# Four chained attention layers on one core: statistics and queue order changed in the second and third layer

## The chip, the cores and the metric

The kernel runs on one core of a Trainium2 chip. The metric is the device time of one execution in microseconds (us). The core has engines that run side by side, each with its own queue of instructions taken strictly in order: TensorE (PE in the rows; its weight loads are PEld), VectorE (DVE), ScalarE (ACT), GpSimd (POOL) and SyncE (SP), which issues transfers. They meet only through semaphores: an instruction that waits holds up all that is queued behind it on its engine.

## The reference, cut to what matters

Input `x` (8, 256, 512) passes through four layers; `u` is a context of the same shape. The first layer (attention) and the fourth are not touched by the change; nor is the third layer's last part (a feed-forward block).

Second layer, for each batch element (a recurrent block, 32 heads of size 16):

```python
xa = ln(x); sx = shifted(xa) - xa
t = tanh((xa + sx*maa_x) @ maa_w1)            # then five mixtures m = t @ maa_w2
xw, xk, xv, xr, xg = (xa + sx*(maa_j + m_j))  # five inputs
w = exp(-exp(time_decay + tanh(xw @ decay_w1) @ decay_w2))
r, k, v, g = xr@Wr.T, xk@Wk.T, xv@Wv.T, silu(xg@Wg.T)
s = k v' + w s ; out = r (faaaa k v' + s)     # a scan over 256 positions
x = x + (groupnorm(out)*gn_w + gn_b) * g @ Wo.T
xc = ln(x); kk = relu(xk2 @ fWk.T)**2; x = x + sigmoid(xr2 @ fWr.T) * (kk @ fWv.T)
```

Third layer: two attentions with 16 heads of 32, the first over `x` itself, the second with keys and values from `u`, each `x + softmax(mask(q k'/sqrt(32))) v @ Wo` after a layer norm of `x`.

## The kernel before, in words

The program runs the layers one after the other; each stage clears its semaphores and meets at a barrier. Nothing of one stage lies beside another.

**Second layer (`l1_layer`).** The 8 batch elements are pipelined by an order written out by hand, one list for each engine. In step b of `ALL` (-1 to 8) three elements are in work: p = b+1 is being prepared (norm, mixtures, projections), b is being scanned in 8 units (`PER`), and c = b-1 is finished (group norm, `Wo`, second norm, feed-forward part). VectorE does for each unit a `spread` (L1535, k times v), a `scan` (L1543) and a `receive` (L1551, times r), with the other operations of p and c between them at fixed places. TensorE's `picks(n)` (L1040) sums a unit's result. All of TensorE's other outputs go through a ring of six PSUM banks in the order of the list `ring`: each label waits until the label six places before it was drained.

The norm of element p: VectorE's `stats(p)` (L729, L733) behind scan 8b; then GpSimd's `deviations` with four instructions (L1009 variance plus eps, L1010 minus the mean, L1012 the power -1/2, L1014 their product); then ScalarE's `normed(p)` (L1271); TensorE turns it (L1088); ScalarE's `turned(p)` (L1281) writes `xa`; VectorE's `shift(p)` (L1561) behind scan 8b+1 needs it. Then ScalarE's `first_part` (L1290), VectorE's `first_input` (L1565), TensorE's `first` (L1096, L1098) and ScalarE's `tanh` (L1299), and the mixtures (L1109, L1315). The norm of c goes the same way: `add_out` (L1620) and `stats_c` behind scan 8b+3, `deviations`, `normed_c` (L1381), the turn, `turned_c` (L1391), `shift_c` (L1633) behind scan 8b+4, `shifts_c` (L1399) and `key_input` (L1637). Its group norm: `centre` (L1144), `squares` (L1365), `variances` (L1151), `roots` (L1375), `inverse` (L1596), `spread_rs` (L1160), `scale_y` (L1604). `out_part` (L1648, L1652) closes the step. `bonus_v` (L1589) needs TensorE's `bonus` (L1056).

**Third layer's attentions (`l2_attentions`).** 16 slots (element, first or second attention), each with 4 groups of 4 heads: 64 steps k. `product_of(k)` gives each step one product of 512 by 256 in two halves: k, v, q of the next slot, then the output product p of the slot before (L1994, L1998). TensorE's step: product half 0, scores(k+1) (L1933), weigh_values(k-2) (L1968), probabilities of k-1 turned for heads 0 and 1 (L1944), product half 1, heads 2 and 3, the sums turned (L1953), and in 24 of the 64 steps a block of normed `x` or of `u` turned for a later slot (`turn_in`, L2016). ScalarE does exponentials (L2042), copies the turned probabilities out (L2049), drains the products k and q (L2066) and the turned `u` (L2077). VectorE does mask (L2121), maxima (L2128), reciprocals (L2135), outputs (L2142), products v and p (L2156, L2159), the turned `x` (L2187) and the norms. These TensorE outputs use a ring of four banks: the second half of a product has the bank of its first half.

## Time and profile before

| what | value |
|---|---|
| time, median of 3 runs | 4052.76 us (4042.41 to 4058.26) |
| the profiled execution, its own time | 4049.53 us |
| its span in the profile | 4047.7 us |
| busy shares of the span | TensorE 86%, VectorE 57%, ScalarE 41%, GpSimd 7% |
| second layer, from its first scan to the end of its last | 1585.1 to 2526.9 us |
| its six steps with all three elements in work (b = 1 to 6) | 1683.6 to 2441.8 us |
| third layer's attentions, from about the third step on | 2640 to 3495 us |

All times in the rows are us from the span's start unless marked ns. PEclk is the clock that TensorE was granted, as a share of 2.4 GHz; the other level is 1.2 GHz. Matmuls in f32 are recorded in two pieces each, so 8 matmuls count x16. Pieces overlap their neighbours slightly, so start to start is the measure of what one costs in a queue.

### The profile page before, as it was taken

What the parts mean: (1) busy time and instruction counts of PE and PEld (TensorE: products, weight loads), DVE (VectorE), ACT (ScalarE), POOL (GpSimd) and SP (SyncE); (2) the same over time, 40 slices, a digit from 0 to 9 for tenths busy, and PEclk for the clock granted to TensorE, in tenths of its full rate; (3) what the DMA queues carried; (4) which work ended last, traced back from release to release, by engine and by line L of the source; (5) the groups of instructions that cost most, each with busy time, mean ns of one, the idle gap of its engine ahead of it and who ended that gap; (6) DMA issues with size and microseconds to landing.
All of it is one profiled execution on the core that took longest, in us unless ns stands there. A gap on an engine that the chain in (4) does not pass through costs nothing. (4 is left out here: it accounts for less than half of the span.)

```text
span 4047.7 us, 52713 instructions
## 1 busy us (share of the span) xinstructions
PE 3495.5 (86%) x20272; PEld 2497.6 (62%) x20272; DVE 2314.6 (57%) x3706; ACT 1667.4 (41%) x3920; POOL 299.5 (7%) x352
## 2 busy tenths in 40 slices
PE   7999999999999936688787976688888888699987
PEld 6777777778777715455454653365555555377764
DVE  5655555555655554887777888255555555442213
ACT  4454444444444423334434342155555555332211
POOL 0000000000000001011101110000000000000000
PEclk9999999999999977898888888799999999799998
DMA  5323121311221025333333333300000000110013
GB/s 195 138 84 121 68 105 74 115 63 63 97 92 63 32 96 165 94 74 89 84 84 88 69 87 75 125 24 6 6 14 19 27 14 14 64 60 27 26 38 104
DMA packets 91123, 291.69 MB, mean 72 GB/s; under 512 B 19872, under 2 KB 28064, under 8 KB 66304
## 3 DMA queue, kind: packets, MB, share of 16 engines
q1 hardware_dynamic: 63152, 182.55, 15.3%
q0 software_dynamic: 10368, 75.50, 5.0%
q10 hardware_dynamic: 17360, 30.32, 2.1%
q8 instruction: 162, 2.65, 0.3%
q14 instruction: 81, 0.66, 0.1%
HBM read 233.82 MB, written 54.53 MB: 71 GB/s over the span
## 5 line engine op out<-in xcount | busy, mean ns | idle before, releaser
L447 ACT ACTIVATE l_prob<-l_bank,l_nmax 128x512 f32<-128x512 f32 x512 | 345.3, 687 | 214.7 <-DVE l_nmax L527 214.7
L527 DVE TENSOR_REDUCE l_nmax<-l_bank 128x1 f32<-128x512 f32 x512 | 318.1, 684 | 80.3 <-PE l_bank L375 80.3
L344 PE MATMUL l_bank<-l_x_hi,l_w_hi 128*128 128x256 f32 x1024 | 316.3, 309 | 16.0 <-DVE l_x_lo L582 16.0
L2042 ACT ACTIVATE l2a_sc<-l2a_sc,l2a_nmax 128x256 f32<-128x256 f32 x512 | 254.5, 506 | 106.2 <-DVE l2a_nmax L2128 106.2
L344 PE MATMUL l_bank<-l_x_hi,l_w_lo 128*128 128x256 f32 x1024 | 291.1, 284 | 0.0
L344 PE MATMUL l_bank<-l_x_lo,l_w_hi 128*128 128x256 f32 x1024 | 291.1, 284 | 0.0
L1543 DVE TENSOR_TENSOR_SCAN l_kv<-l_wx,l_kv 128x2056 f32<-128x2056 f32 x64 | 283.8, 4434 | 3.1 <-ACT l_wx L1265 3.1
L550 DVE COPY l_probT<-l_bank 128x512 f32<-128x512 f32 x256 | 173.8, 689 | 178.5 <-PE l_bank L389 177.3
L389 PE MATMUL l_bank<-l_ident,l_prob 128*128 128x128 f32 x2048 | 248.9, 276 | 11.6 <-DVE l_q_lo L535 6.6
L389 PEld LDWEIGHTS l_bank<-l_ident,l_prob 128*128 128x128 f32 x2048 | 225.5, 141 | 27.1 <-DVE l_k_lo L543 11.4
L2049 ACT ACTIVATE l2a_probT<-l2a_bank 128x512 f32<-128x512 f32 x256 | 144.6, 594 | 224.5 <-PE l2a_bank L1944 224.5
L411 PE MATMUL l_bank<-l_probT,l_v 128*64 128x512 f32 x1024 | 233.8, 598 | 0.0
L344 PEld LDWEIGHTS l_bank<-l_x_hi,l_w_hi 128*128 128x128 f32 x1024 | 197.8, 193 | 31.4 <-issue 31.4
L344 PEld LDWEIGHTS l_bank<-l_x_hi,l_w_lo 128*128 128x128 f32 x1024 | 197.8, 193 | 14.8 <-issue 14.8
L344 PEld LDWEIGHTS l_bank<-l_x_lo,l_w_hi 128*128 128x128 f32 x1024 | 197.7, 193 | 0.0
L469 ACT ACTIVATE l_probT<-l_bank 128x512 f32<-128x512 f32 x256 | 153.1, 598 | 96.8 <-PE l_bank L389 96.8
L2128 DVE CUSTOM_DVE_ANT_0 l2a_sc<-l2a_sc,l2a_mb 128x256 f32<-128x256 f32 x512 | 190.0, 428 | 0.0
L2455 DVE TENSOR_TENSOR l2b_h_lo<-l2b_hf,l2b_h_hi 128x512 fp32r<-128x512 f32 x64 | 44.3, 692 | 230.0 <-ACT l2b_h_hi L2399 229.9
L1994 PE MATMUL l2a_bank<-l2a_xT,l2a_w_q 128*128 128x256 f32 x512 | 129.5, 411 | 49.8 <-ACT l2a_q L2066 36.6
L453 ACT ACTIVATE l_k_hi<-l_bank 128x512 fp32r<-128x512 f32 x64 | 38.3, 598 | 288.1 <-PE l_bank L344 288.1
L2121 DVE SCALAR_TENSOR_TENSOR l2a_sc<-l2a_bank,l2a_m 128x512 f32<-128x512 f32 x256 | 155.8, 673 | 0.0
L1535 DVE TENSOR_TENSOR l_kv<-l_vb,l_ik 128x2048 f32<-128x2048 f32 x64 | 145.5, 2274 | 13.5 <-ACT l_ik L1322 11.5
(273 smaller groups left out, 7638.9 us busy)
## 6 DMA issues: line engine op xcount, KB each, us to landing
l_vb<-vd SPq DMA_DIRECT2D x64, 1024.0 KB
l_w_hi<-kept_w_hi POOLq DMA_DIRECT2D x24, 1024.0 KB, 7.5
l_w_lo<-kept_w_lo POOLq DMA_DIRECT2D x24, 1024.0 KB, 9.7
l_wv_hi<-kept_wv_hi POOLq DMA_DIRECT2D x12, 1024.0 KB, 5.0
l_wv_lo<-kept_wv_lo POOLq DMA_DIRECT2D x12, 1024.0 KB, 7.1
l_wraw<-in_l_wqk SPq DMA_DIRECT2D x8, 1024.0 KB, 9.2
kept_w_hi<-l_w_hi SPq DMA_DIRECT2D x8, 1024.0 KB, 11.5
kept_w_lo<-l_w_lo SPq DMA_DIRECT2D x8, 1024.0 KB, 13.0
```

Of the source, the lines that this page charges most:

```text
L344: mm = pe.matmul(s.ap[:, c * ROWS:(c + 1) * ROWS], a[:, kt, c, g, :], b[:, kt, c * ROWS:(c + 1) * ROWS], start=m == 0, stop=m == 3 * KT - 1)
L389: mm = pe.transpose(s.ap[:, it * P:(it + 1) * P], prob[h][:, it, j * P:(j + 1) * P], ident[:, :])
L411: mm = pe.matmul(s.ap[own, :], v[l][:, pair % 2, j, own], probT[h][:, j, :], start=j == 0, stop=j == IT - 1)
L447: act.activation(prob[h][:, it, :], s.ap[:, :], ACT.Exp, bias=nmax[:, n % 2, it, h:h + 1], accum_out=rsum[:, n % 2, it, h:h + 1]).then_inc ...
L469: act.activation(probT[1][:, j, :], s.ap[:, :], ACT.Copy).then_inc(s.drained, 1)
L527: dve.tensor_reduce(nmax[:, n % 2, it, h:h + 1], s.ap[:, :], AX.X, ALU.max, negate=True).then_inc(max_ready, 1)
L550: dve.tensor_copy(probT[0][:, j, :], s.ap[:, :]).then_inc(s.drained, 1)
L1535: dve.tensor_tensor(kv[n % NK][:, :, 1:ROWS + 1], vb[n % NV][:, :, :], ik[:, ct, :].unsqueeze(1).to_broadcast([P, NJ, ROWS]), ALU.mult).th ...
L1543: dve.tensor_tensor_scan(own, wx[n // 2 % 2][:, :, :].rearrange("p j t -> p (j t)"), own, 0.0, ALU.mult, ALU.add)\
L2042: ins = act.activation(to[:, r, :], to[:, r, :], ACT.Exp, scale=-1.0, bias=nmax[:, k % SC_RING, i, r:r + 1], accum_out=rsum[:, k % SC_RING ...
L2121: dve.scalar_tensor_tensor(out=sc[k % SC_RING][i][:, :, :], in0=s.ap[:, :].rearrange("p (r j) -> p r j", r=RT), scalar=HD ** -0.5, in1=m[: ...
L2128: dve.tensor_tensor_reduce(out=to[:, r, :], in0=to[:, r, :], in1=mb[:, r, :], scale=-1.0, scalar=3.0e38, op0=ALU.add, op1=ALU.min, accum_o ...
```

## The change

In the second layer the statistics of element p+1 are taken one step earlier (unit 7 of the step before), VectorE itself adds eps and negates the mean, GpSimd keeps one power for each norm, and ScalarE multiplies the mean by it. `normed(p)` comes second in ScalarE's step. TensorE turns the normed `x` before `centre`, spreads the group norm's roots before `first`, turns `xc` before the g projection, and does fk before decay_out and the mixture r, fr before picks 5, fv before picks 6. ScalarE and the ring follow. On VectorE, `stats_c` follows `add_out` at once and the mixture g moves behind the spread. In the third layer TensorE's step begins with the four turned probabilities and sums of k-1; values are weighed for k-1, not k-2; `turn_in` comes ahead of product half 1; ScalarE copies all four turned probabilities before the exponentials; the mask of k+1 is made at the end of VectorE's step k; the turned `u` is drained by VectorE.

```diff
 # l1_layer, ring of six banks
+        ring += [f"cen{c}_0", f"cen{c}_1", f"var{c}", f"rsb{c}_0", f"rsb{c}_1"] if c is not None else []
+        ring += [f"t{p}", f"mv{p}_0", f"mv{p}_1"] if p is not None else []
...
 # GpSimd
-                    pool.tensor_tensor(dev[:, :], stats[:, :, 1], eps[:, :], ALU.add).then_inc(ready, 1)
-                    pool.tensor_tensor(bias[:, :], stats[:, :, 0], minus[:, :], ALU.mult).then_inc(ready, 1)
-                    pool.wait_ge(ready, 4 * t + 2)
                     pool.tensor_tensor(dev[:, :], dev[:, :], power[:, :], ALU.pow).then_inc(ready, 1)
-                    pool.wait_ge(ready, 4 * t + 3)
-                    pool.tensor_tensor(bias[:, :], bias[:, :], dev[:, :], ALU.mult).then_inc(ready, 1)
...
 # TensorE
                     if c >= 0:
                         add_bonus(c, 3)
-                        centre(c)
                     if p < B:
                         pe.wait_ge(xn_ready, p + 1)
                         turn(f"xT{p}", x)
                     if c >= 0:
+                        centre(c)
                         variances(c)
-                    if b < B:
+                    if now:
                         picks(PER * b)
-                    if p < B:
-                        if p == 0:
-                            pe.wait_ge(first_in, 32)
-                        first(p)
                     if c >= 0:
                         spread_rs(c)
                     if p < B:
                         if p == 0:
+                            pe.wait_ge(first_in, 32)
                             pe.wait_ge(w2_in, 48)
+                        first(p)
                         mixture(p, "v")
...
                         mixture(p, "w")
-                        project(p, "g")
                     if c >= 0:
                         pe.wait_ge(cxn_ready, c + 1)
                         turn(f"xc{c}", tmp_rows)
                     if now:
                         picks(PER * b + 3)
                     if p < B:
+                        project(p, "g")
                         mixture(p, "k")
                         decay_in(p)
...
 # ScalarE, both norms
-                    act.wait_ge(dev_ready, 4 * (p + 1))
+                    act.wait_ge(dev_ready, p + 1)
+                    for r in range(RT):
+                        ins = act.activation(nb[:, r:r + 1], nb[:, r:r + 1], ACT.Copy, scale=sd[:, r:r + 1])
+                    ins.then_inc(nb_ready, 1)
+                    act.wait_ge(nb_ready, p + 1)
...
                         start_state(PER * b + 1)
+                    if p < B:
+                        normed(p)
+                    if now:
                         ...
                         project(b, "r", 1, ir)
-                        spread_w(b, 1)
                     if c >= 0:
                         take_y(c)
                     if p < B:
-                        normed(p)
+                        turned(p)
                     if c >= 0:
                         squares(c)
-                    if p < B:
-                        turned(p)
-                    if c >= 0:
                         roots(c)
+                    if now:
+                        spread_w(b, 1)
...
 # VectorE, both norms
+                    dve.wait_ge(var_ready, p + 1)
+                    dve.tensor_scalar(sd[:, :], mv[:, :, 1], EPS, None, ALU.add)
+                    dve.tensor_scalar(nb[:, :], mv[:, :, 0], -1.0, None, ALU.mult).then_inc(dev_in, 1)
...
-                        if n == 0 and p < B:
-                            stats(p)
                         if n == 3 and c >= 0:
                             add_out(c)
-                        if n == 3 and p < B:
-                            mix(p, "g")
+                            stats_c(c)
+                        if n == 7 and p + 1 < B:
+                            stats(p + 1)
                         if 0 <= unit + 1 and b < B:
                             spread(unit + 1)
-                        if n == 3 and c >= 0:
-                            stats_c(c)
+                        if n == 3 and p < B:
+                            mix(p, "g")
...
 # l2_attentions, ring of four banks
+        ring += [f"t{k - 1}_{i}" for i in Q4] + [f"r{k - 1}"] if quad else []
         ring += [f"{what}{z}_0"] if what else []
+        ring += [f"o{k - 1}"] if quad else []
+        ring += [f"{turned}T{to}_0", f"{turned}T{to}_1"] if turned else []
         ring += [f"{what}{z}_1"] if what else []
...
 # TensorE
+                    if 0 <= k - 1 < K:
+                        for i in Q4:
+                            turn_probs(k - 1, i)
+                        turn_sums(k - 1)
                     product(k, 0)
                     if 0 <= k + 1 < K:
                         scores(k + 1)
-                    if 0 <= k - 2 < K:
-                        weigh_values(k - 2)
                     if 0 <= k - 1 < K:
-                        turn_probs(k - 1, 0)
-                        turn_probs(k - 1, 1)
+                        weigh_values(k - 1)
+                    turn_in(k)
                     product(k, 1)
-                    if 0 <= k - 1 < K:
-                        turn_probs(k - 1, 2)
-                        turn_probs(k - 1, 3)
-                        turn_sums(k - 1)
-                    turn_in(k)
...
 # ScalarE
-                    turned_u(k)
+                    if 0 <= k - 1 < K:
+                        for i in Q4:
+                            probs(k - 1, i)
+                        sums(k - 1)
                     if 0 <= k < K:
                         exponentials(k, 0)
-                    if 0 <= k - 1 < K:
-                        probs(k - 1, 0)
+                    product(k, 0)
                     if 0 <= k < K:
                         exponentials(k, 1)
-                    ...
                         exponentials(k, 2)
                         exponentials(k, 3)
                     product(k, 1)
...
 # VectorE: order of a step after
+                    norm(k, "rows")
+                        for i in Q4:
+                            maxima(k, i)
+                    product(k, 0)
+                        mask(k + 1)
+                        outputs(k - 1)
+                    turned(k)
+                    norm(k, "stats")
                     cross_mask(k)
+                        reciprocals(k)
                     product(k, 1)
```

## Rows read from the trace of the kernel before

**Rows 1.** Windows: us, then busy us of each engine, PEclk, DMA share, GB/s.
```profile
1585.10:1683.60 98.50, 69.25 (x355) 49.80 (x353) 88.15 (x45) 33.08 (x63) 9.62 (x4) 0.83 0.40 95
...
1935.50:2062.80 127.30, 103.37 (x461) 67.80 (x461) 101.38 (x65) 49.72 (x93) 18.34 (x8) 0.87 0.34 83
...
2640.00:3495.00 855.00, 743.22 (x4773) 498.87 (x4772) 470.55 (x1628) 459.64 (x1476) 73.32 (x106) 0.97 0.04 13
```
**Rows 2.** VectorE's waits, step b = 3: total us, times, longest.
```profile
DVE l_tmp L1648 <- PE l_bank L1076: 6.1, 2, 3.3
DVE l_sx L1561 <- ACT l_xa L1281: 5.9, 1, 5.9
DVE l_sxc L1633 <- ACT l_xc L1391: 5.6, 1, 5.6
DVE l_y L1604 <- PE l_bank L1160: 4.6, 2, 4.4
```
**Rows 3.** TensorE's waits in the same step.
```profile
PE l_bank L1088 <- ACT l_x L1271: 7.4, 1, 7.4
PE l_bank L1096 <- DVE l_xf L1565: 6.7, 1, 6.7
PE l_bank L1088 <- ACT l_tmp L1381: 6.0, 1, 6.0
```
**Rows 4.** GpSimd's groups, second layer: count, busy us, mean ns, idle before.
```profile
L1014 POOL TENSOR_TENSOR l_nb<-l_nb,l_sd 128x2 f32<-128x2 f32 x7 | 26.0, 3712 | 0.6
...
L1012 POOL TENSOR_TENSOR l_csd<-l_csd,l_power 128x2 f32<-128x2 f32 x7 | 12.2, 1749 | 0.6
```
**Rows 5.** Timeline of second layer, steps b = 1 and 3: start, us, what.
```profile
1712.11 3.75 PE L1096 MATMUL l_bank<-l_xf,l_w 128*128 128x256 f32 x8 [7.04 <-DVE l_xf L1565]
...
1715.79 3.00 PE L1098 MATMUL l_bank<-l_xf,l_w 128*32 128x256 f32 x8
...
1985.03 7.07 PE L1066 MATMUL l_bank<-l_xf,l_w_Wv 128*128 128x256 f32 x32
...
1993.47 1.99 PE L1109 MATMUL l_bank<-l_tT,l_w2a 32*128 32x256 f32 x8
...
2024.70 3.78 PE L1109 MATMUL l_bank<-l_tT,l_w2a 32*128 32x256 f32 x8
```
**Rows 6.** VectorE's groups in step b = 3.
```profile
L1543 DVE TENSOR_TENSOR_SCAN l_kv<-l_wx,l_kv 128x2056 f32<-128x2056 f32 x8 | 35.5, 4434 | 0.0
L1551 DVE TENSOR_TENSOR l_kv<-l_kv,l_ir 128x2048 f32<-128x2048 f32 x8 | 18.3, 2281 | 0.0
```
**Rows 7.** VectorE's wait in the step b = 7, 2441.8 to 2526.9.
```profile
DVE l_sxc L1633 <- ACT l_xc L1391: 6.2, 1, 6.2
```
**Rows 8.** TensorE's waits from 2640 to 3495 us.
```profile
PE l2a_bank L1994 <- ACT l2a_q L2066: 36.6, 15, 2.4
PE l2a_bank L1994 <- ACT l2a_k L2066: 34.2, 14, 2.4
PE l2a_bank L1994 <- DVE l2a_xT L2187: 22.6, 14, 1.7
PE l2a_bank L1994 <- ACT l2a_uT L2077: 7.9, 8, 1.0
```
**Rows 9.** TensorE's timeline, a step with the product v, and a slow product.
```profile
3034.02 1.09 PE L1944 MATMUL l2a_bank<-l2a_ident,l2a_sc 128*128 128x128 f32 x8
3034.95 3.60 PE L1998 MATMUL l2a_bank<-l2a_w_v,l2a_xT 128*128 128x512 f32 x8
...
3048.64 5.41 PE L1994 MATMUL l2a_bank<-l2a_xT,l2a_w_q 128*128 128x256 f32 x16 [2.44 <-ACT l2a_q L2066]
```
**Rows 10.** ScalarE's groups, 16 steps of the attentions (2773 to 2990 us).
```profile
L2042 ACT ACTIVATE l2a_sc<-l2a_sc,l2a_nmax 128x256 f32<-128x256 f32 x127 | 63.1, 506 | 25.6 <-DVE l2a_nmax L2128 25.6
L2049 ACT ACTIVATE l2a_probT<-l2a_bank 128x512 f32<-128x512 f32 x64 | 36.2, 594 | 58.4 <-PE l2a_bank L1944 58.4
...
L2066 ACT ACTIVATE l2a_k<-l2a_bank,l2a_vec 128x256 f32<-128x256 f32 x16 | 6.7, 472 | 7.4 <-PE l2a_bank L1994 7.4
```

More of the change, by code:

```diff
@@ L860, in l1_layer @@
         ident = ph.sb("ident", [P, P])
-        eps, power, minus = [ph.sb(name, [P, RT]) for name in ("eps", "power", "minus")]
+        eps, power = [ph.sb(name, [P, RT]) for name in ("eps", "power")]
         scrap = ph.sb("scrap", [P, 1])
@@ L1232, in _ @@
                         rows(f"fr{c}", sxc, W["fWr"])
+                    if now:
+                        picks(PER * b + 5)
                     if p < B:
                         project(p, "k")
-                    if 0 <= b < B:
-                        add_bonus(b, 2)
-                        picks(PER * b + 6)
                     if c >= 0:
@@ L1242, in _ @@
                         rows(f"fv{c}", xc, W["fWv"], 1)
+                    if now:
+                        add_bonus(b, 2)
+                        picks(PER * b + 6)
                     if p < B:
@@ L1377, in normed_c @@
                 def normed_c(c):
-                    act.wait_ge(cdev_ready, 4 * (c + 1))
+                    act.wait_ge(cdev_ready, c + 1)
                     full(act, S[f"var{c}"])
+                    for r in range(RT):
+                        ins = act.activation(cnb[:, r:r + 1], cnb[:, r:r + 1], ACT.Copy, scale=csd[:, r:r + 1])
+                    ins.then_inc(cnb_ready, 1)
+                    act.wait_ge(cnb_ready, c + 1)
                     for r in range(RT):
@@ L1485, in _ @@
                         start_state(PER * b + 5)
+                    if c >= 0:
+                        turned_c(c)
+                    if now:
                         spread_w(b, 3)
@@ L1669, in _ @@
                             gate_y(c)
-                        if n == 2 and 0 <= b < B:
+                        if n == 2 and now:
                             bonus_v(b)
@@ L1693, in _ @@
                             mix(p, "r")
-                        if 0 <= b < B:
+                        if now:
                             receive(unit)
-                        if n == 0 and 0 <= b < B:
+                        if n == 0 and now:
                             bonus_rk(b)
@@ L2068, in product @@
                     ins.then_inc(s.drained, 1)
-                def turned_u(k):
-                    what, z = turns_at_end(k - 1)
-                    if what != "u":
-                        return
-                    for half in range(2):
-                        s = S[f"uT{z}_{half}"]
-                        full(act, s)
-                        act.activation(uT[:, 2 * half:2 * half + 2, :], s.ap[:, :].rearrange("p (c t) -> p c t", c=2), ACT.Copy)\
-                            .then_inc(s.drained, 1)
                 def store(k):
@@ L2159, in product, with norm @@
                         dve.tensor_tensor(to[:, half, :], s.ap[:, :], to[:, half, :], ALU.add).then_inc(s.drained, 1)
-                def norm(k):
+                def norm(k, only):
                     what, z = norm_of(k)
-                    if what is None:
+                    if what != only:
                         return
@@ L2176, in norm, with turned @@
                         norm_rows(dve, src, mv, sd, xn, xn_ready)
-                def turned_x(k):
-                    what, z = turns_at_end(k - 1)
-                    if what != "x":
+                def turned(k):
+                    what, z = turns_at_end(k)
+                    if what is None:
                         return
```

113 lines of the change are left out of this document (47 added, 66 removed).

## The prediction

> **What bounds the kernel now.** I read first the windows over the stretches that the change touches [rows 1]. In a full step of the second layer VectorE is busy for 101.4 of 127.3 us and TensorE for 103.4: neither is full, each waits for the other in turn. In the third layer's attentions TensorE is busy for 743.2 of 855 us while VectorE and ScalarE stand at 55%: TensorE's queue sets the pace, and what can be won there is its idle 112 us. Second the waits. In the second layer VectorE loses 5.9 us before `shift`, 5.6 before `shift_c`, 4.6 before `scale_y` and 6.1 in `out_part`, 22.2 of its 25 idle us in step b = 3 [rows 2]. TensorE waits in the same step 7.4 us for the normed x, 6.7 for `first`'s input and 6.0 for the second norm [rows 3]. Both norm chains go through GpSimd: four instructions on 128x2 elements, one of which lasts 3.7 us because it ends only with VectorE's scan [rows 4, 6]. In the attentions four waits make 36.6 + 34.2 + 22.6 + 7.9 = 101.3 us [rows 8], so they are nearly all of the 112.
>
> **Second layer, a full step.** I lay the new lists out from the start of scan 8b, with 4.4 us for a scan, 2.2 to 2.3 for receive and spread [rows 6], and TensorE's project r still running until about +7 (7.1 us for a projection [rows 5], queued behind the last picks).
> - The statistics now end in unit 7 of the step before, and the power needs at best about 0.7 and at most the 3.7 us of the longest GpSimd row; one row stands at 1.75 [rows 4], which I take. It is hidden behind receive 7 and `out_part` in any case. `normed` starts at +2, x is turned at about +9, `xa` is complete at about +12, and `shift` comes at +14.4 (scan, spread, receive, the product r k, scan). The 5.9 us go, with 2.5 us to spare.
> - `centre` comes 2 us later than it could (the turn is ahead of it), so `roots` ends at about +17 and VectorE waits 1.5 us for it where it waited 0.5.
> - The roots are spread before `first`: ready at +21, `scale_y` at +24. The 4.6 us go. But `first`, mixture v, picks and `bonus` now follow later: from +22, with 3.75 + 3.0 us for `first` [rows 5], 0.9 for tanh, 2.0 for a mixture, 1.1 for picks and 1 for half a bonus, `bonus_v` can start at +34, and VectorE is there at +31.7. A new wait of 2.5 us, between 0 (if `first` runs at full clock, about half as long) and 4.
> - `stats_c` directly behind `add_out`, one power instead of four instructions, and the turn of xc ahead of projection g: `xc` is ready at about +61.5, VectorE asks at +66. The 5.6 us go. Projection g (7.1) and mixture k (2.0) now stand between that turn and ScalarE's `shifts_c`, which follows its mixture k in the list: it ends at about +73.8, `key_input` could start at +69.4. A new wait of 4.4 us; bounds 0 and 7.
> - `out_part` and the wait for k: fk and fr come about 5 us earlier relative to VectorE, and fv stands before picks 6. I keep 0.9 us of 6.1; bounds 0 and 6.
> - Added work: four operations on VectorE of 128x2 (a few tenths of a us in all) and four on ScalarE, which has 77 idle us in a step [rows 1]. Also the cover that receive and spread gave to `deviations` is no longer needed.
> Sum: VectorE's own 102 us plus 0.4 plus 1.5 + 2.5 + 4.4 + 0.9 = about 112 us. TensorE's own is 127.3 less some 24 us of waits [rows 1, 3], 103 us, so it fits under that, though not by much. The six full steps last 758.2 us, 126.4 each: 6 x 14.4 = 86 us. Step b = 0 has only the first norm chain (98.5 us [rows 1]) and gives back some 5; b = 7 has only the second, with its wait of 6.2 [rows 7], and gives 5. The pipeline's filling and draining I put at nothing: there GpSimd is not held up by a scan, and what it loses ScalarE and VectorE gain. Second layer: -96 us.
>
> **Third layer.** The waits of 2.44 us for q and k come from the bank ring: half 1 of a product takes the bank of half 0, and ScalarE drains that late, behind the copies [rows 9]. In the new ring half 1 takes another bank, or, where a block is turned in, the same bank but 2 to 3 us later. The waits for xT and uT stood where a turned block was needed by the next instruction; now half 1 (3.6 us) and the next head of probabilities (two blocks of 0.93, start to start [rows 9]) lie between. All four go: -101.3 us. One product in each eight steps ran at the lower clock behind such a wait, 5.41 us instead of 3.6 [rows 9]; seven of these would be 12 us, I count half, -6.
> What could be late now is the head of the step: four blocks turned, which need all exponentials of k-1 and TensorE may not start without them. From the step's start: the head 2.1 us, product half 0 to +5.7; ScalarE has copied the four blocks (0.59 each), drains half 0 (0.9) and does three pairs of exponentials (1 us a head) until +9.5 [rows 10]; the next head is due at +11.4 (a step of (855 - 107)/64 = 11.7 on average). It fits by 2 us. VectorE's maxima are done by +4.6, its mask by +9, the reciprocals by +11.4, the copy on GpSimd by +12.4, and the sums are turned at +13.3. VectorE takes the turned u from ScalarE, 1.4 us in 8 of 64 steps, hidden. I leave 0.1 us a step for waits that just touch: +6. Third layer: -101 us; bounds -112 (no idle) and -50 (a touch of 0.9 us in each step).
>
> **Sum.** -96 - 101 = -197 us against the profiled execution's 4049.5 (span 4047.7, so 1.8 lie around it): 3852.5. The median shown is 3.2 us above that execution: 3856 us.
>
> **The clock.** The second layer's windows show 0.83 to 0.87 of the full clock, the attentions 0.97 [rows 1]; in b = 3 a mixture takes 3.78 us soon after the 6.0 us wait, and 1.99 before it [rows 5]. The Trainium skill, in "TensorE: Matmul & The Clock Gate", section "The HAM clock gate", says that the throttled state is the default and that activity releases it. By that rule a TensorE that waits 8 us a step instead of 24 would lose its slow stretches. That result stands as a rival below: `first` takes 3.5 us, the wait at `bonus_v` goes, and a step ends at 109.5 us, 15 us less over six steps; in the sum above I left `first` slow.
>
> **Rivals.**
> - *The second layer's waits only move.* For it: TensorE's own 103 us and VectorE's 102 stand in a loop through ScalarE, and I find three new waits already. If `bonus_v`, `key_input` and `out_part` take their upper bounds 4, 7 and 6, a step is 120.5: 35 us won plus 10, total -146, 3907 us.
> - *The head of the third layer's step waits for the exponentials.* For it: one late head delays the whole queue, and 2 us is the only slack. If the 29 steps that waited for q or k wait 2.4 us as before and only xT and uT go: -30, total -126, 3927 us. Against it: ScalarE is idle for 46% of the stretch [rows 1].
> - *The clock stays up* (above): 3841 us.
> - *Slower.* The ring and the head make a serial loop: if ScalarE's exponentials (end at +9.5) end behind the step's last matmul, TensorE stands still while it drains. The price is a step of head 2.1, product 3.6, drain 0.9, exponentials 3, then scores, values and half a product 5.6, and 0.4 of signals, 15.6 us against 13.4: 64 x 2.2 = +141, less 96, 4100 us. It decides only from +11.4 on. I see nothing in the rows that adds 2 us there.
> - *The change does not do it*: the late value is a transfer or another engine's, not the named one. Against it, each wait above names a releaser that moves. 4045 us.
>
> **How the numbers follow.** Forecast as worked out 0.60, waits move in the second layer 0.16, late head 0.10, clock stays up 0.08, slower 0.02, no effect 0.04. Predicted 3856. The range takes the bounds of both layers: low 3812 (steps of 109.5 and no idle in the attentions give 3830; 18 us less if the wait at `key_input` is 1.4 instead of 4.4), high 3932 (the late head's case). A measurement tells about 0.5%, 20 us, from no change. Faster by more than that 0.94, within it 0.04, slower 0.02.
>
> **What would show it.** Scans of neighbouring steps 112 us apart; no idle before L1561, L1604 and L1633 (the lines of `shift`, `scale_y`, `shift_c`, shifted by the edit); new idle before `bonus_v` and `key_input`; one GpSimd power for each norm. In the attentions no waits before the second halves, 8 steps in 94 instead of 109 us, TensorE busy over 97%. I am wrong on the second layer if steps stay above 120, and on the third if the turned probabilities show waits for the exponentials.

## The result and the profile after

The changed kernel takes 3786.91 us (median of 4 runs, 3785.54 to 3791.47); the kernel before, on the same chip, 4047.59 us (4 runs, 4040.05 to 4058.26). The ratio is 0.9353, with a 95% interval of 0.9333 to 0.9374. The forecast was 3856 us with a range of 3812 to 3932: the direction is right, the size is 69 us too small, and the time lies below the range.

The profiled execution has a span of 3789.7 us, against 4047.7: 258.0 us less. By stage, in us:

| stretch | before | after | difference | forecast |
|---|---|---|---|---|
| second layer, b = 0 | 98.5 | 93.6 | -4.9 | -5 |
| its six full steps | 758.3 | 642.1 | -116.2 | -86 |
| b = 7 | 84.9 | 79.2 | -5.7 | -5 |
| draining behind it | 73.8 | 73.3 | -0.5 | 0 |
| third layer's attentions | 913.1 | 779.5 | -133.6 | -101 |
| all else | 2119.1 | 2122.0 | +2.9 | 0 |

First the windows, as in [rows 1]: us, busy us of TensorE, its weight loads, VectorE, ScalarE and GpSimd, PEclk, DMA share, GB/s. The lines are step b = 0, step b = 3, the six full steps, and the attentions from about the third step on.

```profile
1584.90:1678.40 93.50, 70.58 (x355) 51.08 (x353) 88.20 (x46) 34.80 (x69) 2.66 (x1) 0.84 0.44 100
1893.80:2001.80 108.00, 98.28 (x468) 64.92 (x467) 101.49 (x69) 50.67 (x97) 5.32 (x2) 0.94 0.42 98
1678.40:2320.50 642.10, 576.12 (x2731) 377.88 (x2732) 607.46 (x403) 301.95 (x577) 29.27 (x11) 0.94 0.41 98
...
2510.00:3240.00 730.00, 718.00 (x4812) 487.48 (x4811) 510.17 (x1650) 448.08 (x1464) 74.00 (x106) 0.99 0.05 16
```

VectorE's own 101.5 us in step b = 3 are the 101.4 of before; what shrank is its idle time, from 25.9 us to 6.5. TensorE is now busy for 718 of 730 us in the attentions. These are VectorE's waits in the six full steps (total, times, longest), to be held against [rows 2]:

```profile
DVE l_y L1648 <- ACT l_y L1402: 19.8, 6, 4.4
DVE l_ruk L1597 <- PE l_bank L1053: 6.9, 10, 1.9
DVE l_tmp L1659 <- PE l_bank L1073: 3.1, 4, 2.1
DVE l_kv L1540 <- DVE l_ruk L1597: 1.5, 6, 0.2
```

Nothing waits before `shift` (now L1569), `inverse` (L1604), `scale_y` (L1612) and `shift_c` (L1644). The first two lines are the waits that the forecast named as new, `key_input` (3.3 us a step) and `bonus_v` (1.15). TensorE's waits in step b = 3 [rows 3] are short as well:

```profile
PE l_bank L1157 <- DVE l_rs L1604: 3.2, 1, 3.2
PE l_bank L1085 <- ACT l_tmp L1384: 2.8, 1, 2.8
...
PE l_bank L1093 <- DVE l_xf L1573: 0.9, 1, 0.9
```

The timeline of step b = 3 (start, us, what) gives the second norm's chain, its projection g and what VectorE does meanwhile, and `first`, which is still slow in this step [rows 5]:

```profile
1914.32 3.75 PE L1093 MATMUL l_bank<-l_xf,l_w 128*128 128x256 f32 x8 [0.85 <-DVE l_xf L1573]
1918.00 2.45 PE L1095 MATMUL l_bank<-l_xf,l_w 128*32 128x256 f32 x8
...
1949.52 1.93 ACT L1394 ACTIVATE l_xc<-l_bank,l_vecc 128x256 f32<-128x256 f32 x4 [1.16 <-PE l_bank L1085]
...
1952.07 7.74 PE L1063 MATMUL l_bank<-l_xf,l_w_Wg 128*128 128x256 f32 x32
...
1962.49 1.70 ACT L1402 ACTIVATE l_y<-l_sxc,l_vecc 128x256 f32<-128x256 f32 x4
...
1964.22 1.23 DVE L1648 TENSOR_TENSOR l_y<-l_y,l_xc 128x1024 f32<-128x1024 f32 x1 [3.60 <-ACT l_y L1402]
```

`xc` is ready at 1951.4 and `shifts_c` (L1402) starts only at 1962.5, behind projection g and mixture k. GpSimd keeps one power per norm instead of four instructions [rows 4] (count, busy us, mean ns, idle before):

```profile
L1010 POOL TENSOR_TENSOR l_csd<-l_csd,l_power 128x2 f32<-128x2 f32 x6 | 16.0, 2661 | 304.8 <-DVE l_cnb L1636 304.8
L1010 POOL TENSOR_TENSOR l_sd<-l_sd,l_power 128x2 f32<-128x2 f32 x5 | 13.3, 2661 | 252.0 <-DVE l_nb L1563 252.0
```

In the attentions I compare the 48 steps between the scores of step 9 and those of step 57: 655.7 us before, 554.8 after. TensorE's waits there were 85.4 us before, of the four kinds of [rows 8]; after, there is none, and the window is full:

```profile
2744.16:3399.87 655.71, 570.38 (x3706) 383.77 (x3705) 363.05 (x1243) 349.68 (x1118) 60.24 (x84) 0.99 0.04 15
```
```profile
2609.95:3164.73 554.78, 554.78 (x3706) 378.08 (x3705) 393.69 (x1257) 338.63 (x1104) 60.30 (x84) 1.00 0.05 17
```

In these steps a slow product as in [rows 9] is not found any more. One step of the timeline, with the turned probabilities and sums at its head and the two halves of a product q:

```profile
2812.37 1.91 PE L1954 MATMUL l2a_bank<-l2a_ident,l2a_sc 128*128 128x128 f32 x16
2814.12 0.38 PE L1963 MATMUL l2a_bank<-l2a_ident,l2a_rows 128*128 128x128 f32 x2
2814.34 3.62 PE L2004 MATMUL l2a_bank<-l2a_xT,l2a_w_q 128*128 128x256 f32 x16
...
2819.96 3.72 PE L2004 MATMUL l2a_bank<-l2a_xT,l2a_w_q 128*128 128x256 f32 x16
```

Half 1 of the product q follows its neighbours without the 2.44 us wait. ScalarE's work of [rows 10] is what it was (exponentials 513 ns instead of 506); its idle time has shrunk.

### The profile page after: what moved, and what is told of

The parts are those of the page before. It is cut to its first block and busy times, and to the rows that moved or that the text cites. A ratio compares the mean times of both kernels' runs of the same rounds, so it can differ in the third digit from the quotient of the medians.

```text
span 3789.7 us, 52731 instructions
## 1 busy us (share of the span) xinstructions
PE 3434.3 (91%) x20272; PEld 2464.7 (65%) x20272; DVE 2352.3 (62%) x3754; ACT 1660.2 (44%) x3936; POOL 205.1 (5%) x303
## 5 line engine op out<-in xcount | busy, mean ns | idle before, releaser
L344 PE MATMUL l_bank<-l_x_hi,l_w_hi 128*128 128x256 f32 x1024 | 316.2, 309 | 15.8 <-DVE l_x_lo L582 15.8
L2112 DVE SCALAR_TENSOR_TENSOR l2a_sc<-l2a_bank,l2a_m 128x512 f32<-128x512 f32 x256 | 158.6, 680 | 102.7 <-PE l2a_bank L1943 102.7
L344 PEld LDWEIGHTS l_bank<-l_x_hi,l_w_hi 128*128 128x128 f32 x1024 | 197.8, 193 | 31.3 <-issue 31.3
L2119 DVE CUSTOM_DVE_ANT_0 l2a_sc<-l2a_sc,l2a_mb 128x256 f32<-128x256 f32 x512 | 214.4, 481 | 0.0
L344 PEld LDWEIGHTS l_bank<-l_x_hi,l_w_lo 128*128 128x128 f32 x1024 | 197.8, 193 | 14.8 <-issue 14.8
L2056 ACT ACTIVATE l2a_probT<-l2a_bank 128x512 f32<-128x512 f32 x256 | 132.2, 608 | 139.5 <-PE l2a_bank L1954 139.5
L2385 ACT ACTIVATE l2b_hf<-l2b_bank,l2b_b 128x512 f32<-128x512 f32 x64 | 44.0, 688 | 254.7 <-PE l2b_bank L2328 254.7
L411 PEld LDWEIGHTS l_bank<-l_probT,l_v 128*64 128x64 f32 x1024 | 67.8, 136 | 132.6 <-issue 132.6
```

What stands on the lines that cost most here:

```text
L344: mm = pe.matmul(s.ap[:, c * ROWS:(c + 1) * ROWS], a[:, kt, c, g, :], b[:, kt, c * ROWS:(c + 1) * ROWS], start=m == 0, stop=m == 3 * KT - 1)
L411: mm = pe.matmul(s.ap[own, :], v[l][:, pair % 2, j, own], probT[h][:, j, :], start=j == 0, stop=j == IT - 1)
L2056: act.activation(probT[k % 2][i][:, :, :], s.ap[:, :].rearrange("p (j i) -> p j i", j=RT), ACT.Copy).then_inc(s.drained, 1)
L2112: dve.scalar_tensor_tensor(out=sc[k % SC_RING][i][:, :, :], in0=s.ap[:, :].rearrange("p (r j) -> p r j", r=RT), scalar=HD ** -0.5, in1=m[: ...
L2119: dve.tensor_tensor_reduce(out=to[:, r, :], in0=to[:, r, :], in1=mb[:, r, :], scale=-1.0, scalar=3.0e38, op0=ALU.add, op1=ALU.min, accum_o ...
```

## The experiments

All times are medians; a ratio is to the kernel before, run on the same chip along with it, with its 95% interval. "Full" is the six full steps, "attentions" the stage, "steady" its 48 steps, all from the profile. Before has 758.3, 913.1 and 655.7, after 642.1, 779.5 and 554.8.

**1. Which layer.** `l1_only` has only the second layer of the change, `l2_only` only the attentions.

```diff
 l1_only: def l1_layer         from the changed kernel, all else before
 l2_only: def l2_attentions    from the changed kernel, all else before
```

> Second layer of the changed kernel, all else as before. Theory (the two layers' gains are independent, each stage stands alone behind a barrier): the second layer's full steps last 107 us as in the changed kernel, total 127 us less than before, about 3921. Rival (part of the 261 us comes from one layer's effect on the next, through transfers or the clock): the two partial kernels' gains add up to clearly less than the whole, this one is above 3935.

> Third layer of the changed kernel, all else as before. Theory: attentions in 780 us instead of 913, total 133 us less than before, about 3915. Rival as for the other part: above 3930.

`l1_only`: 3931.95 us, ratio 0.9702 (0.9666 to 0.9738), full 642.1. `l2_only`: 3910.71 us, ratio 0.9654 (0.9620 to 0.9689), attentions 780.1, full 757.5. Each layer's length is that of the full change, to 0.6 us, whatever stands ahead of it. The medians give -113.8 and -135.0, together 12 us less than the change: the attentions that `l1_only` left untouched took 927.9 us in its profile, not 913.1 (see the last section). For the same reason `l1_only` missed its 3921 by 11 us.

**2. Second layer: statistics and power, or TensorE's order.** `stats_only` is the kernel before with the early statistics and the single power alone. `late_stats` is the changed kernel with the statistics of p back behind scan 8b. `rs_late` is the changed kernel with `spread_rs` behind `first` again.

```diff
 stats_only (against before)
-                        if n == 0 and p < B:
-                            stats(p)
+                        if n == 7 and p + 1 < B:
+                            stats(p + 1)
 ... and the new GpSimd, ScalarE and VectorE pieces of both norms
 rs_late (against after), TensorE and ring
+                    if p < B:
+                        ...
+                        first(p)
                     if c >= 0:
                         spread_rs(c)
...
-                        first(p)
                         mixture(p, "v")
```

> Kernel before, with only the early statistics and one GpSimd power for each norm (VectorE adds eps and negates, ScalarE multiplies); all queues of TensorE and the place of the normed x in ScalarE's queue as before. Theory of the prediction (the norm chains through GpSimd are the larger half): the waits before shift (5.9) and shift_c (5.6) go, full steps about 115 us, total 75 to 85 us less. Rival (TensorE's order is what holds the steps): the waits reappear before scale_y and in out_part, full steps stay above 121, total less than 40 us won.

> Changed kernel, with the first norm's statistics back behind scan 8b (still one power). Theory: GpSimd's power then ends about 9 us after the step's start, the turn of x stands ahead of centre in TensorE's queue, xa is complete at about 15 us; shift waits 1 to 3 us and inverse about as long: full steps 110 to 112 instead of 107, 20 to 30 us over the changed kernel. Rival (the unit ahead is worth nothing once only one power is left): full steps of 107, same time as the changed kernel.

> Changed kernel, second layer: TensorE spreads the group norm's roots behind first again (ring order too). The early statistics alone gave steps of 112.6 us and the whole change gives 107.0, so TensorE's reordering is worth 5.6 us a step. Theory A (this move carries it): scale_y waits again, 4 to 6 us, bonus_v waits less, full steps 110 to 112. Theory B (the second norm's turn ahead of projection g carries it): steps stay within 1 us of 107.

`stats_only`: 3963.20 us, ratio 0.9793 (0.9756 to 0.9829), full 674.5: 84 of the 116 us come from here; TensorE's order, with what follows it on the other engines, brings the other 32. No run has the single power without the early statistics. What is left are the waits that it takes:

```profile
DVE l_y L1613 <- PE l_bank L1158: 33.8, 12, 5.5
DVE l_tmp L1660 <- PE l_bank L1074: 24.1, 12, 2.7
```

The waits of `shift` and `shift_c`, 35.3 and 33.7 us before in six steps, are gone but for 2.0: the turn of xc stands behind projection g here and yet nothing waits for it, so GpSimd's four instructions, and not the place of the turn, made `shift_c` late.

`late_stats`: 3805.69 us, 0.9400 (0.9366 to 0.9434), full 658.7, +16.6. VectorE's waits in six steps sum to 44.6 instead of 31.3 us: `bonus_v` 9.8, `inverse` 3.5, and 6.5 ahead of the product of r and k (L1588), with no releaser shown. `shift` itself doesn't wait, against the 1 to 3 us that I had expected. Late statistics delay the whole chain behind them by a little, not the one use.

`rs_late`: 3798.81 us, 0.9368 (0.9333 to 0.9403), full 655.6, +13.5. `scale_y` waits for 32.1 us in six steps, as before the change, but `key_input`'s wait falls from 19.8 to 7.2 and `bonus_v`'s 6.9 are gone, so only part of it is paid. VectorE's waits in `rs_late`:

```profile
DVE l_y L1616 <- PE l_bank L1159: 32.1, 12, 5.3
DVE l_y L1652 <- ACT l_y L1406: 7.2, 6, 1.4
```

**3. Second layer: the clock.** Filler products of 128x256 (their number of columns is `ROWS`, 256) go ahead of the instructions at which TensorE waits; the real product overwrites their bank. From step b = 2 on, `fill_before` has eight of them at each of three places of the kernel before (the turn of x, `first`, the turn of xc), `fill_after` six ahead of `spread_rs` in the changed one.

```diff
+                def fill(label, n):
+                    free(pe, S[label])
+                    for _ in range(n):
+                        pe.matmul(S[label].ap[:, 0:ROWS], heads[:, 0, :], W["Wo"][:, 0, 0:ROWS], start=True, stop=True)
```

> Kernel before, with 8 f32 matmuls of 128x256 on constants (results never used, overwritten in the bank that TensorE is about to claim) put where TensorE waits in the second layer: ahead of the wait for the normed x, ahead of first, ahead of the wait for the second norm. Nothing else moves. Theory A (TensorE's lower clock behind these waits is on the path: mixture r 3.78 us, fk 9 us): granted clock of the six full steps rises from 0.86 to above 0.95, the waits in out_part and for k (8.7 us a step together) shrink, full steps about 121 instead of 126.4, 30 us less. Theory B (the clock is beside the path, the time is in the waits' order): the clock rises, steps stay at 125 to 127.

> Changed kernel, second layer: 6 f32 matmuls of 128x256 on constants (results overwritten) where TensorE waits for the roots, ahead of spread_rs. Theory A (first still runs at half clock, 3.75 + 2.45 us, because of that wait, and bonus_v waits for it): half-clock time of the six full steps falls from 82 to under 50 us, first takes 3.5 us, the wait at bonus_v goes, steps about 105.5. Theory B (as in the kernel before, the clock is beside the path): half-clock time falls, steps stay at 106.5 to 107.5.

`fill_before`: 4041.33 us, 0.9987 (0.9972 to 1.0003): no difference. It did raise the clock. The six full steps of before, then of `fill_before`:

```profile
1683.60:2441.80 758.20, 611.77 (x2738) 399.86 (x2739) 608.35 (x385) 297.64 (x556) 110.02 (x48) 0.86 0.35 83
```
```profile
1684.10:2434.20 750.10, 653.75 (x2979) 435.74 (x2980) 608.08 (x385) 296.65 (x556) 110.00 (x48) 0.91 0.34 84
```

The time at 1.2 GHz fell from 212 to 137 us, and the steps won 8.2 us, more than they vary where nothing in them was changed (757.0 to 758.7 in `l2_only`, `ring_only` and `ring_turn`). VectorE waits for `shift` and `shift_c` as long as before (35.2 and 33.7 us): these waits come through GpSimd and ScalarE, and the higher clock didn't shorten them. Eight fillers at a place don't keep the clock up in every step either: of the five with fillers `first` still takes 5.3 to 6.8 us in four, and 3.8 in one. `fill_after`: 3778.61 us, 0.9318 (0.9284 to 0.9353), full 632.9, with 51 us at 1.2 GHz instead of 82. It wins 9.2 us in the stretch; `bonus_v`'s wait goes from 6.9 to 0.7 us. There `first` takes 3.8 us in the five steps that have fillers, as the clock's rival wanted. So the slow stretches did cost something: what the fillers took away was worth 1.4 and 1.5 us a step, less than the 2.5 of the rival. These are net figures, since the fillers take time of their own. At `fill_before`'s rate the 130 us less at 1.2 GHz that came with the change would be 14 of its 116 us, an estimate.

**4. Second layer: the remaining waits.** `g_first` puts projection g ahead of the turn of xc again. `shifts_early` leaves the turn and puts ScalarE's `shifts_c` between the two halves of g, with `bonus` ahead of the picks of scan 1; it also has the late mask of 6.

```diff
 g_first (against after), TensorE; ring and ScalarE's turned_c alike
                         mixture(p, "w")
+                        project(p, "g")
                     if c >= 0:
                         pe.wait_ge(cxn_ready, c + 1)
                         turn(f"xc{c}", tmp_rows)
...
-                        project(p, "g")
```

> Changed kernel, second layer: projection g back ahead of the turn of xc on TensorE and ahead of turned_c on ScalarE (ring order too). Theory A (this move is worth little or costs: it brought the new wait of 3.6 us at key_input): the key_input wait goes, a wait of 1 to 4 us before shift_c comes, steps 105 to 108. Theory B (it carries the 5.6 us): full steps 110 or more, shift_c waits 5 us or more.

> Changed kernel with three moves: the mask of step k at the head of VectorE's step (13 us less by its own run), ScalarE's shifts_c between the two halves of projection g instead of behind mixture k, and TensorE's bonus ahead of picks 1. Theory (the new waits at key_input, 3.3 us a step, and bonus_v, 1.2 us, are on VectorE's path): both go or shrink to under 1 us, full steps 103 to 104, total 18 to 24 us under the kernel with the late mask alone, about 3757. Rival (TensorE has taken over as the bound, its waits only close up): steps stay above 106.

`g_first`: 3769.48 us, 0.9296 (0.9261 to 0.9330), full 625.1, 17 us less than after. This part of the change costs time. VectorE's waits in its six steps:

```profile
DVE l_ruk L1598 <- PE l_bank L1053: 6.8, 8, 2.0
DVE l_tmp L1660 <- PE l_bank L1073: 4.0, 5, 2.4
...
DVE l_sxc L1645 <- issue: 1.0, 3, 0.3
DVE l_y L1649 <- ACT l_y L1402: 0.9, 3, 0.3
```

The 19.8 us of `key_input` are gone but for 0.9, and `shift_c` waits for 1.0 us in six steps, not the 1 to 4 us a step that I had expected. `shifts_early`: 3770.67 us, 0.9297 (0.9270 to 0.9323), full 633.6. Here `key_input` and `bonus_v` wait for 3.4 and 1.9, but `out_part` for 16.1 instead of 3.1: of 21.4 us of waits, 13.0 have only moved. Its steps of 105.6 us lie between the two cases of its expectation.

**5. Third layer: what won.** `ring_only` is the kernel before with two banks exchanged: half 1 of a product and the third turned block. `ring_turn` also puts `turn_in` ahead of half 1, with its drains in the same step; in the 24 steps that turn a block the two banks are not exchanged there, since the turned block stands between the halves.

```diff
 ring_only (against before)
+        second, third = f"{what}{z}_1", f"t{k - 1}_2"
+        if second in bank and third in bank:
+            bank[second], bank[third] = bank[third], bank[second]
 ring_turn (against ring_only), ring and TensorE
-        if second in bank and third in bank:
+        if second in bank and third in bank and turns_at_end(k)[0] is None:
...
+                    turn_in(k)
                     product(k, 1)
...
-                    turn_in(k)
```

> Kernel before, third layer: only the banks of product half 1 and of the third turned probability exchanged, so that half 1 no longer has the bank of half 0; no queue reordered. Theory (the 2.44 us waits for q and k are that bank's drain by ScalarE): these 29 waits, 71 us, go, and with them the one slow product in eight steps; eight steps about 98 us instead of 109, total 75 to 85 us less. Rival (half 1 only moves its wait: ScalarE's queue is late anyway and the turned probabilities behind it wait instead): less than 30 us.

> The kernel before with the two banks of the third layer's scores and products exchanged (ring_only) and the turn of the next unit's x put ahead of product half 1. ring_only left waits of 16.5 us (xT) and 4.1 us (uT) between 2700 and 3240 and 619.8 us for scores 9 to 57. Theory that the third layer's gain is ring plus turn: these two waits go, 9 to 57 comes to about 590, total 30 us under ring_only: 3965 to 3972. Rival: TensorE meets the next wait instead (probT or the eviction of the other half), and the total is within 10 us of ring_only: 3990 to 4000; then the order within a step with the probabilities at its head is what matters.

`ring_only`: 3999.54 us, 0.9888 (0.9868 to 0.9908), steady 619.8. `ring_turn`: 3985.17 us, 0.9835 (0.9812 to 0.9858), steady 609.6. TensorE's waits over the 48 steps of the first, then the second:

```profile
PE l2a_bank L2004 <- ACT l2a_probT L2055: 25.5, 24, 1.1
PE l2a_bank L2000 <- DVE l2a_xT L2193: 19.8, 12, 1.7
PE l2a_bank L2000 <- ACT l2a_uT L2083: 5.8, 7, 0.8
```
```profile
PE l2a_bank L2004 <- ACT l2a_probT L2055: 25.3, 24, 1.1
PE l2a_bank L2022 <- DVE l2a_xn L748: 21.8, 12, 1.8
```

The exchange took the 58.6 us of waits for q and k and made a new one of 25.5: a product v or p now meets a bank whose turned probabilities ScalarE hasn't copied. Moving the turn took the waits for xT and uT and made one of 21.8 for the normed rows, which VectorE has ready too late for it. Both edits found the next wait, as the rival of `ring_turn`'s expectation said, though both times lie between the two cases of their expectations (48 us won by the first, 3985 us for the second). The change removes that too. By its lists this is because its head gives ScalarE the turned probabilities first, and VectorE's step begins with the norm's rows; no run takes these two apart. Of 100.9 us, the ring brings 36, the turn 10, and the rest of the reordering 55. The ring's 36 would be 46 to 49 against the longer lengths of the unchanged code (last section).

**6. Third layer: the head's slack, and the mask.** `mask_late` is the changed kernel with the mask of step k made in step k, ahead of the maxima. `act_load` adds ten copies of 128x128 to ScalarE's step, between the exponentials.

```diff
 mask_late (against after), VectorE
+                        ...
+                        mask(k)
                         for i in Q4:
                             maxima(k, i)
...
-                        mask(k + 1)
 act_load (against after), ScalarE
+                        for j in range(10):
+                            act.activation(extra[:, j, :], ident[:, :], ACT.Copy)
                         exponentials(k, 1)
```

> Changed kernel, third layer: the mask of step k back at the head of VectorE's step k instead of the end of step k-1. Theory (in the steady part TensorE's queue is full and VectorE has slack; only the last steps without products, 6.1 us each, are a loop through VectorE and ScalarE): eight steps stay at 92.3 us, the last three steps grow back to 8 to 11 us, total 8 to 15 us over the changed kernel. Rival (the early mask carries the steady part): the exponentials come too late for the head, eight steps above 96 us, 30 us or more.

> Changed kernel, third layer: ten more copies of 128x128 (about 2.4 us, results never used) on ScalarE in each step, between product half 0 and the last three heads' exponentials. Theory (the head of TensorE's step has about 2 us of slack in steps with k and q, more in the others): the exponentials end 0.5 us or so after the head could start, in half of the steps; 64 steps grow by 10 to 40 us. Rival (the slack is large, ScalarE is idle for 40% of the time): no change, under 5 us. Rival (no slack is left): 64 times 2.4, 150 us.

`act_load`: 3790.91 us, 0.9368 (0.9349 to 0.9387). ScalarE is busy for 433 us instead of 339 in the 48 steps, 2.0 us more in each (I had put 2.4), and these don't grow:

```profile
2612.43:3167.20 554.77, 554.77 (x3705) 378.06 (x3704) 395.89 (x1257) 433.35 (x1584) 60.28 (x84) 1.00 0.05 17
```

So the head has at least 2.0 us of slack; the late head and the serial loop of the forecast decided nothing. `mask_late`: 3778.39 us, 0.9338 (0.9319 to 0.9357), against my expectation of a loss. The steady steps are the same 554.8; the first nine take 92.8 us instead of 101.4, the last ones 3.6 more, the stage 774.5 instead of 779.5. The whole kernels' intervals overlap, so only the stage's 5.0 us are seen, in one profile. The early mask wins nothing in the middle, since TensorE is full there with either.

**7. Together.** `best_plain` is the changed kernel with `g_first`, `mask_late` and `bonus` ahead of the picks of scan 1; `best_fill` adds the six fillers (of 256 columns here too).

> The changed kernel with three moves: projection g stands ahead of the turn of xc on TensorE again (g_first), the mask's product is back where it was before the change in the third layer (mask_late), and bonus stands ahead of the picks of scan 1 (as in shifts_early). If the key_input wait and the late mask add, g_first's 17 us and mask_late's 8 us give 3787 - 25 = 3762 us, with steps of 103 to 105 and the bonus_v wait (6.8 us in six steps with g_first) under 3: then 3757 to 3762. Rival: VectorE is the bound already at 104, moving bonus only shifts a wait to out_part: 3764 to 3770, and six full steps no shorter than 625 us.

> best_plain with six filler products of 512 columns ahead of spread_rs in each step (their bank is overwritten by the real product). Theory: the half clock left in the second layer (61 us in six steps with g_first) still costs something: cold falls to about 40, 3 to 9 us less than best_plain: 3750 to 3755. Rival: at 104 us per step VectorE sets the pace alone, so the fillers change nothing (within 3 us of best_plain), or cost 2 us per step where they stand ahead of spread_rs (+12).

`best_plain`: 3754.46 us, 0.9262 (0.9242 to 0.9281), faster than the changed kernel (0.9333 to 0.9374) and a little under the 3757 that I had expected at best. `best_fill`: 3749.87 us, 0.9258 (0.9239 to 0.9278), the same. The six full steps of `best_plain`, and the two longest of VectorE's waits in them:

```profile
1676.00:2292.20 616.20, 560.01 (x2731) 372.09 (x2732) 606.64 (x403) 301.72 (x577) 29.28 (x11) 0.96 0.44 101
```
```profile
DVE l_tmp L1660 <- PE l_bank L1073: 2.6, 4, 0.7
DVE l_ruk L1598 <- PE l_bank L1053: 2.1, 5, 0.9
```

VectorE is busy for 606.6 of 616.2 us: it is the bound, with steps of 102.7 us, and so the fillers have nothing left to win (619.3 us).

## Why the prediction missed

**The bound and the releasers: right.** TensorE's queue in the attentions, two engines waiting in turn in the second layer, the norm chains through GpSimd. The eight named waits of [rows 2, 8] behaved as said: `out_part` kept 0.5 us a step, one wait of 3.4 us for xT is left at the attentions' start, and the others went. Steps b = 0 and b = 7 came out within 1 us of their 5.

**Second layer, statistics: right, nearly to the us.** From the start of scan 8b (1893.8) the forecast had x turned at +9, `xa` complete at +12 and `shift` at +14.4. The trace has +9.0 (the turn runs from 1901.8 to 1902.8), +10.6 and +14.2. The power takes 2.66 us, not the 1.75 chosen, and is hidden as said.

**The sum of the new waits: too large.** This is the first failed step. "A new wait" of 1.5 at `inverse`, 2.5 at `bonus_v`, 4.4 at `key_input` and 0.9 in `out_part` made 9.3 us; measured in six steps are 0, 1.15, 3.3 and 0.5, 5.0 in all. The 1.5 fell because `roots` ends at +14.8, not +17: `centre` takes 1.88 us right behind the turn. From there on the chain runs ahead of my layout by a little more than VectorE does. `first` starts at +20.5, not +22, and its second part takes 2.45 us, not 3.00; `bonus_v` can start at +31.6, not +34, and is asked for at +29.7, not +31.7; `key_input` can start at +70.4, not +73.8, and is asked for at +66.8, not +69.4. A step is 101.2 us busy, 5.2 of waits (with the 0.25 ahead of `spread`) and 0.6 of small gaps, 107.0, where the forecast had 102.4 and 9.3, 111.7: 6 x 4.7 = 28 of the 30 us missed.

**The clock as a rival: it came in part.** Less time at 1.2 GHz did follow (212 to 82 us in the six steps, PEclk 0.86 to 0.94). The page "TensorE: Matmul & The Clock Gate" of the Trainium skill, section "The HAM clock gate", says that activity releases the throttle, and the trace agrees. The sum had left `first` slow, and it is in b = 3; but over the six steps it takes 4.5, 6.1, 6.1, 4.9, 3.8 and 4.9 us from its first to its last matmul, against 5.3 to 6.7 before. In the two steps with 6.1 us `bonus_v` waits for 2.0 and 2.1 us, near the 2.5 of the sum; in the one with 3.8 it doesn't wait, and that step is the shortest, 105.0 us. So part of what the sum of new waits had too large, some 1 us a step at `bonus_v`, is this rival's doing; its step of 109.5 us was too long all the same. `fill_before` shows the size: 75 us less at 1.2 GHz were worth 8 us. My reading is that most of it lay where TensorE was early anyway.

**Third layer: the waits right, the rest of the stage left out.** This is the second failed step. In the 48 steady steps all 85.4 us of waits went, as forecast. Beside them TensorE's busy time fell by 15.6 us where I had put -6 and +6: the products q, slow behind a wait, give 9 of it (17 us of these steps lay at 1.2 GHz before, none do after); the other 7, by my reckoning, are the overlap with the neighbour that each of 43 stops had broken, about 0.2 us a stop. The touches (+6) did not exist, and `act_load` fits that: the head has 2 us to spare. Eight steps take 92.5 us, near the forecast's 94.

The other 33 us came at the stage's ends, where I had counted only their share of the four waits, 101.3 - 85.4 = 16. The first nine steps won 7.1. Behind the scores of step 57 the stage takes 87.8 us instead of 113.8. TensorE's waits there before:

```profile
PE l2a_bank L1933 <- DVE l2a_sc L2121: 6.2, 3, 3.4
PE l2a_bank L1994 <- ACT l2a_k L2066: 2.4, 1, 2.4
PE l2a_bank L1994 <- ACT l2a_q L2066: 2.4, 1, 2.4
```

They and their like sum to 15.8 us and are 4.8 after, and TensorE's busy time in this stretch falls from 90.0 to 75.4 us, with PEclk from 0.91 to 0.99. TensorE is at 1.2 GHz for 2 us of it instead of 21. The early masks give 3.6 of these 26 us (`mask_late`); that values weighed one step sooner give most of the rest is my reading, and no run shows it. The prediction had looked at the steady stretch and never at the last six steps.

**The rest of the 69 us.** The spans differ from the forecast by 61 us, which these two steps make up in the main. The other 8 lie in the medians: the forecast put its own 3.2 us above the profiled run, and the measured one lies 4.6 below it.

**The range: its low end didn't take its own bounds.** VectorE's 102.4 us alone in each full step give -144 instead of -86, the attentions without idle -112 instead of -101; from 3856 that is 3787. That this is the measured time is luck: the second layer's six steps won 116 of these 144 us, and the attentions 134 where this bound has 112, since its idle time was not all that they could lose. The text named both bounds and combined them only with new waits of 1.5 and more. `best_plain` reached that step (102.7 us). Against its chances: the case that got 0.60 had the right mechanism, and of the rivals' only the clock's occurred, in part.

## What to carry to other kernels

Where a change takes away named waits, the floor is the own time of the engine that then sets the pace: put it into the range, with all bounds taken at once. Cost the filling and draining of a pipeline apart from its steady steps: here 33 of the attentions' 133.6 us lay there. And a reordering is several edits: here one of them (the turn ahead of projection g) cost 17 us inside a gain of 116, and only undoing them one by one showed it.

## What the runs showed of the hardware

- *A low clock can be nearly free.* Fillers took away 75 and 31 us at 1.2 GHz in six steps and won 8.2 and 9.2 us, their own time included. It costs where something waits for the slow instruction: of the 9.2 us, 6.2 are `bonus_v`'s wait for `bonus`, behind `first`.
- *The same code has several lengths, by its time at 1.2 GHz.* The attentions of before took 913.1 us in its own profile and 927.9, 925.3 and 924.8 in those of `l1_only`, `fill_before` and `stats_only`, which have them unchanged. Their 48 steps take 655.7, 668.6, 665.4 and 665.4 us. TensorE's waits in them are the same, 85.4 us; its time at 1.2 GHz is 17, 44, 38 and 38 us, and the steps grow by about half of what that grows by. `l1_only` has

```profile
2615.61:3284.24 668.63, 583.30 (x3706) 392.99 (x3705) 361.48 (x1243) 349.52 (x1118) 59.60 (x84) 0.97 0.04 14
```

  What sets how long the low clock lasts is open, so a difference between two such stages is good to some 15 us only, the 133.6 of this change included. With no waits the length repeats: the 48 steps take 554.8 us in the changed kernel and in all ten others that have its order of TensorE there.
- *GpSimd beside VectorE.* The power of 128x2 takes 2.66 us where it starts with VectorE's `spread` (2.29 us, two inputs) and 0.69 alone. The page "GPSIMD Engine Reference" of the Trainium skill, section "Specifications", says that GpSimd's interfaces to SBUF, the on-chip memory, are shared with VectorE and contended for by its instructions with two inputs from there, and the trace agrees.
- *And VectorE beside GpSimd.* With the early mask VectorE's maxima (two inputs from SBUF) take 489 ns on average, instead of 430 before and 420 in `mask_late`, 23 us more of VectorE's busy time than there in the 48 steps. The mean hides different kinds: 12 of the 384 take 2.56 us, 12 take 0.61, and the others 0.42 or less. Each of the slowest 12 starts just behind an addition of GpSimd and ends just behind it; those of 0.61 run beside its copies of 0.49. The first, from the changed kernel's timeline:

```profile
2617.62 2.46 POOL L1927 TENSOR_TENSOR l2a_x<-l2a_x,l2a_b_o 128x1024 f32<-128x1024 f32 x1 [0.82 <-DVE l2a_xn L748]
2617.81 2.56 DVE L2119 CUSTOM_DVE_ANT_0 l2a_sc<-l2a_sc,l2a_mb 128x256 f32<-128x256 f32 x1
```

  In `mask_late` the same addition (2.38 us) runs beside the four masks instead, which read one input from TensorE's bank (`l2a_bank`) and keep their 0.68 us each. So the order of mask and maxima decides what meets GpSimd's addition. Nothing waited for it here.
